# A graph layer with routed experts on one core: routing in two batches, results scattered to a two-row table

## The reference

```python
xs = x[src]
for r in range(4):                                   # relation weights
    msg += (xs @ W_rel[r] + b_rel[r]) * where(edge_type == r, edge_weight, 0)[:, None]
agg = segment_sum(msg, dst) / maximum(segment_sum(edge_weight, dst), 1)
x1  = layer_norm(x + x @ W_self + b_self + agg, ln1)
gnn = layer_norm(x1 + gelu(x1 @ W_ffn1 + b1) @ W_ffn2 + b2, ln2)     # 512 -> 1024 -> 512
x   = x + gnn                                        # gnn is fed the normed x

xt     = norm(x)
probs  = softmax(xt @ router_w.T + router_b)         # 16 experts, the best 2 are kept
out    = sum over e of gate[e] * (gelu(xt @ w1[e].T + b1[e]) @ w2[e].T + b2[e])   # 512 -> 256 -> 512
return x + out
```

## Time and profile before

| | us |
|---|---|
| median of three runs | 641.01 |
| the profiled execution | 639.41 |
| its span | 637.5 |
| PE busy in the span | 526.0 |
| DVE busy | 320.0 |
| POOL busy | 229.9 |
| ACT busy | 119.3 |

### The profile page before, as it was taken

One profiled execution on the slowest core, in us unless ns is written; L12 is line 12 of the kernel. 1 busy time (PEld: TensorE's weight loads), 2 busy tenths in 40 slices (PEclk: granted clock), 3 DMA queues, 4 the chain that ended last, 5 costly groups with the idle time before them and its releaser, 6 DMA issues.

```text
span 637.5 us, 7136 instructions
## 1 busy us (share of the span) xinstructions
PE 526.0 (82%) x2292; PEld 353.1 (55%) x2292; DVE 320.0 (50%) x847; ACT 119.3 (19%) x251; POOL 229.9 (36%) x270
## 2 busy tenths in 40 slices
PE   1999999999965999999999999529359999999300
PEld 1888888887612756656657667223146666666200
DVE  6788563212226145986977995948102222222144
ACT  2121101000111322322223312011022222222000
POOL 3630000037777777777773000004700011110273
PEclk9999999989977999999999999855569999999855
DMA  8427242249898677776774592442534477872285
GB/s 318 185 83 255 113 166 92 90 121 290 278 398 283 195 203 201 200 199 178 200 204 123 201 407 86 155 178 99 207 105 165 164 265 265 293 267 100 85 257 203
DMA packets 47703, 125.54 MB, mean 197 GB/s; under 512 B 6496, under 2 KB 7136, under 8 KB 45360
## 3 DMA queue, kind: packets, MB, share of 16 engines
q0 software_dynamic: 17344, 63.20, 32.3%
q1 hardware_dynamic: 27360, 57.57, 24.1%
q10 hardware_dynamic: 2960, 4.27, 2.3%
HBM read 85.70 MB, written 39.32 MB: 196 GB/s over the span
## 4 chain that ended last, share of the span: by engine, by line
PE 74%; POOL 8%; DVE 7%; issue 5%; DMA 4%; ACT 1%; POOLq 1%; ACTq 0%; SPq 0%; DVEq 0%
PE ps L828 11%; PE ps L839 10%; PE ps L961 8%; PE ps L978 8%; PE ps L762 7%; PE ps L763 7%; PE ps L764 7%; PE ps L794 6%; POOL greg L569 3%; POOL xslot L543 3%; PE ps L954 2%; POOL greg L522 2%; PE ps L805 2%; PE ps L860 1%; DMA x_res<-x 1%
## 5 line engine op out<-in xcount | busy, mean ns | idle before, releaser
L522 POOL DMA_INDIRECT greg<-msg,row_i x157 | 156.7, 998 | 145.0 <-DMA msg<-greg 93.6
L762 PE MATMUL ps<-w_hi,xT_hi 128*128 128x512 f32 x200 | 81.1, 405 | 0.0
L763 PE MATMUL ps<-w_lo,xT_hi 128*128 128x512 f32 x200 | 79.8, 399 | 0.0
L764 PE MATMUL ps<-w_hi,xT_lo 128*128 128x512 f32 x200 | 79.7, 398 | 0.0
L828 PE MATMUL ps<-freg,wreg 128*128 128x256 f32 x320 | 71.7, 383 | 0.8 <-ACT freg L622 0.8
L839 PE MATMUL ps<-wreg,freg 128*128 128x512 f32 x160 | 72.1, 598 | 0.0
L828 PEld LDWEIGHTS ps<-freg,wreg 128*128 128x128 f32 x320 | 60.3, 191 | 16.4 <-issue 7.5
L961 PE MATMUL ps<-wreg,freg 128*128 x224 | 55.7, 393 | 0.0
L978 PE MATMUL ps<-wreg,freg 128*128 x112 | 52.7, 593 | 0.9 <-ACT freg L709 0.9
L794 PE MATMUL ps<-greg,sel 128*32 128x512 f32 x320 | 47.9, 638 | 6.3 <-DMA greg<-msg,row_i 6.3
L543 POOL DMA_INDIRECT xslot<-work,pos_i x20 | 19.7, 986 | 85.2 <-DVE pos_i L1347 79.4
(11 more groups left out here) (170 smaller groups left out, 648.3 us busy)
## 6 DMA issues: line engine op xcount, KB each, us to landing
wreg<-experts POOLq DMA_DIRECT2D x11, 1025.0 KB, 6.3
msg<-greg SPq DMA_DIRECT2D x40, 256.0 KB, 2.0
xslot<-greg SPq DMA_DIRECT2D x1, 8960.0 KB, 25.6
greg<-xslot SPq DMA_DIRECT2D x28, 256.0 KB, 4.1
yslot<-greg SPq DMA_DIRECT2D x28, 256.0 KB, 2.9
wreg<-experts SPq DMA_DIRECT2D x5, 1025.0 KB, 9.6
wreg<-w SPq DMA_DIRECT2D x8, 512.0 KB, 12.7
w_in<-w_rel ACTq DMA_DIRECT2D x3, 1024.0 KB, 6.5
```

The source lines that it names most:

```text
L522: nc.gpsimd.indirect_dma_start(gath[:, c % RING, :], None, msg, bass.IndirectOffsetOnAxis(ap=row_i[:, c:c + 1], axis=0)).then_inc(s_gath[c ...
L762: nc.tensor.matmul(bank(t % 5), xT_hi[:, at], w_hi[:, i, wk], start=(k == 0), stop=False)
L763: nc.tensor.matmul(bank(t % 5), xT_hi[:, at], w_lo[:, i, wk], start=False, stop=False)
L764: mm = nc.tensor.matmul(bank(t % 5), xT_lo[:, at], w_hi[:, i, wk], start=False, stop=(k == KD - 1))
```

## The change

- **Routing** is split in `choose` and `place` and done in two batches, tiles 0 to 5 and tiles 6 to 9. The first batch's routing stands between `other_norms` of tile 7 and of tile 8 on DVE; its exp stands between `copy_xmT` of the fourth pair and `product_out` of tile 8 on ACT; its counts stand between the FFN products of tile 8 on PE. The best two are chosen on the logits, ahead of the exp. `place` takes a first layout of `xslot` from the first batch alone; rows of the second batch that don't fit go behind it. So a block's rows are no longer together, and DVE works out, per block, where its rows are (`trow_i`, from ten wide instructions and as many small ones on 128 partitions).
- **Rows of `xslot`** get four more values: the row's place in the result table, its first expert, and its two gates (`XW = 516`). `xslot` is cleared as soon as the gathers are issued, and one more DMA, behind the clearing, writes 4480 single ids of four bytes into it. `yslot` is gone, and its clearing with it.
- **Experts.** POOL loads each block's rows by an indirect gather (four blocks ahead) and, in place of the store, scatters the results, scaled by their gates on DVE, to a table `results` with two neighbouring rows per node. SP loads all expert weights. DVE works out gate and result row in four small instructions per block (`gates_of`).
- **Combine.** SP loads the results linearly, five loads of two tiles (1 MB); DVE adds both rows; ACT stores the output.
- **Bias product**: gates are turned in three groups with one copy each, and the product uses banks 0, 1, 2 and 4. It stands, as before, between routing and experts on PE. A small gelu on ACT after the exp loads its table early.
- **Nodes.** The bias of the second norm is added to `x_res` by POOL after the self bias (ten additions of 128x512), so that `other_norms` has one instruction less per tile. `sums_out` on ACT makes one copy in place of two, and DVE reads PSUM itself; `window_sums` waits for DVE's low part in place of the copies.
- **Start.** `turn_xn` runs two tiles ahead of the products in place of three.

The core of the diff:

```diff
+            def rows_to_tile(t):
+                if t >= MR:
+                    pool.wait_ge(e_xT, t - MR + 1)
+                    pool.wait_ge(e_prep, 2 * (t - MR + 1))
+                nc.gpsimd.indirect_dma_start(
+                    xs[:, t % MR, :], None, xslot,
+                    bass.IndirectOffsetOnAxis(ap=trow_i[:, t:t + 1], axis=0)).then_inc(e_x[t % MR], 16)
+
+            def tile_to_results(t):
+                pool.wait_ge(e_yt, t + 1)
+                nc.gpsimd.indirect_dma_start(
+                    results, bass.IndirectOffsetOnAxis(ap=node_i[:, t % MR:t % MR + 1], axis=0),
+                    ys[:, t % MR, :], None).then_inc(e_out[t % MR], 16)
+
+            def expert_tiles(first, end):
+                for t in range(first, min(first + AHEAD, end)):
+                    rows_to_tile(t)
+                for t in range(first, end):
+                    tile_to_results(t)
+                    if t + AHEAD < end:
+                        rows_to_tile(t + AHEAD)
+
+            pool.wait_ge(r_fast.sc, 2 * NT * 16)
+            pool.wait_ge(d_rows, 1)
+            expert_tiles(0, USUAL)
...
+            choose(r_fast, fast, cs, 0)
+            place(r_fast, cs, 0)
             other_norms(fast, cs, NT - 2)
             other_norms(fast, cs, NT - 1)
+            choose(r_fast, fast, cs, 1)
+            place(r_fast, cs, 1)
...
+            for g, (a, b) in enumerate(BIAS_TILES):
+                pe.wait_ge(d_gTc, g + 1)
+                for t in range(a, b):
+                    after(pe, d_b2t, t - len(B_BIAS) + 1)
+                    nc.tensor.matmul(bank(B_BIAS[t % len(B_BIAS)]), gT[:, t, :], eb2_s[:, :],
+                                     start=True, stop=True).then_inc(d_b2, 1)
             pe.wait_ge(d_b2t, NT)
...
+            for p in range(PAIRS):
+                sp.dma_start(both[:, 2 * p:2 * p + 2, :],
+                             results[4 * p * P:4 * (p + 1) * P, :].rearrange("(t p c) d -> p t (c d)", t=2, c=2))\
+                    .then_inc(f_in[p], 16)
...
+            for t in range(NT):
+                pool.wait_ge(s_xn, t + 1)
+                nc.gpsimd.tensor_tensor(x_res[:, t, :], x_res[:, t, :], vec[:, V_B2 - V_G1, :], ALU.add).then_inc(s_xb, 1)
```

More of the change, by code:

```diff
@@ new lines, in program @@
+        tval = room(TAB * EXPERTS).rearrange("p (t e) -> p t e", e=EXPERTS)
+        empty_slots = flat(tval)[:, 0:XW]
+        both = wreg[:, 0:2 * NT * D].rearrange("p (t n) -> p t n", t=NT)
+        tbase, texp, tstart, told, tfrom, tlater, tpos = (room(TAB) for _ in range(7))
+        tring = tfrom
+        slot_ids = tpos[:, 0:SLOT_TILES]
+        row16 = sb("row16", [P, 8, EXPERTS])
+        room_old, end_old, at_old, less, room_now, end_now, later_by, change_old = (row16[:, i, :] for i in range(8))
@@ L765, in product @@
                 mm.then_inc(s_prod, 1)
-            for t in range(3):
+            for t in range(2):
                 turn_xn(t)
@@ L905, in _ @@
             logits(fast, PAIRS - 1)
+            counts(r_fast, 1)
             with pe.If(general_wanted(pe)):
@@ L1173, in norm_stats @@
[L1173 to L1177 removed]
+                for s, r in enumerate(rows):
+                    n.did(v.bn_stats(st[:, s, :], r))
@@ new lines, in norm_stats @@
+                sync(n)
+                for s in range(k):
+                    n.did(v.bn_aggr(mv[:, s, :], st[:, s, :]))
+                sync(n)
+                var2, seed, sq, root = nvar[:, 0:k], nseed[:, 0:k], nsq[:, 0:k], nrs[:, 0:k]
+                did(v.tensor_scalar(var2, mv[:, 0:k, 1], EPS, None, ALU.add))
+                n.did(v.tensor_scalar(seed.bitcast(I32), var2.bitcast(I32), 1, None, ALU.logical_shift_right))
+                if k == 1:
+                    n.did(v.tensor_scalar(newton[:, :], nscale[:, :], var2, None, ALU.mult))
@@ new lines, in choose @@
+                did(v.tensor_tensor(lg[:, tiles, 0:EXPERTS], lg[:, tiles, 0:EXPERTS],
+                                    rb_s[:, :].unsqueeze(1).to_broadcast([P, k, EXPERTS]), ALU.add))
+                for t in range(a, z):
+                    n.did(v.max(lg[:, t, EXPERTS:], lg[:, t, 0:EXPERTS]))
+                sync(n)
+                v.tensor_tensor(low[:, tiles, :], lg[:, tiles, :],
+                                lg[:, tiles, EXPERTS:EXPERTS + 1].to_broadcast([P, k, EXPERTS + 8]),
+                                ALU.subtract).then_inc(r.low, 1)
@@ new lines, in choose @@
+                for t in range(a, z):
+                    n.did(v.max_index(i8[:, t, :], lg[:, t, EXPERTS:], lg[:, t, 0:EXPERTS]))
+                sync(n)
+                for c_ in range(2):
+                    n.did(v.tensor_copy(idx_f[:, c_, tiles], i8[:, tiles, c_]))
+                sync(n)
+                for c_ in range(2):
+                    n.did(v.tensor_tensor(choice[:, c_, tiles, :], num[:, 0:EXPERTS].unsqueeze(1).to_broadcast([P, k, EXPERTS]),
+                                          idx_f[:, c_, tiles].unsqueeze(2).to_broadcast([P, k, EXPERTS]), ALU.is_equal))
@@ L1286, in _ @@
                 for t in range(NT):
+                    zs.did(v.tensor_tensor(x_res[:, t, :], x_res[:, t, :], vec[:, V_B2 - V_G1, :], ALU.add))
+                sync(zs)
+                for t in range(NT):
                     after(dve, slow.x1T, t - 3)
@@ L1293, in _ @@
                         other_norms(slow, zs, t)
-                dve.wait_ge(slow.lgt, PAIRS)
+                dve.wait_ge(s_zero, 64)
+                for b in range(len(BATCHES)):
+                    choose(r_slow, slow, zs, b)
+                    place(r_slow, zs, b)
             rd = Steps(d_dve)
```

600 lines of the change are left out of this document (346 added, 254 removed).

## The result

| | before | after |
|---|---|---|
| median, us (4 runs each) | 640.51 | 655.13 |
| lowest to highest | 639.59 to 641.83 | 652.01 to 657.05 |
| ratio of the times, 95% interval | | 1.0222 (1.0177 to 1.0266) |
| span of the profiled execution | 637.5 | 655.3 |
| DVE busy in the span | 320.0 | 342.8 |

What follows compares the result with a forecast made beforehand. PE was taken to bound three quarters of the chain, nearly still before the first expert turn and after the last result. Terms 0.5 - 9.9 + 23.4 - 10.3 = +3.7 on span 637.5 led to 644.7 us, range 630 to 658.

Steps and rivals of the forecast that it cites:

- Start: First products: turning two ahead gains 0, POOL's ten additions slow DVE a little; +0.5 us, bounds 0 and 3.
- Node stage: Node products: DVE's shorter norms and the saved copy lie under a busy PE; 0 us.
- First batch: Routing of tiles 0 to 5: tile 8's norm starts at 401.4 in place of 398.45; scatters and clearing hidden.
- Second batch to T: Routing of tiles 6 to 9: rows known at T = 432.1, 4.7 us earlier than before.
- T to the first turn: Rows known to PE's first expert turn: bias product at half clock ends last, turn at T + 25; routing -9.9 us.
- Loop: Expert loop: take, scatter, gather and landing need 10.56 us for two iterations, where PE wants 8.22; +23.4 us.
- The pauses hide it in two of ten iterations: Expert loop: PE's existing pauses absorb part of the 1.17 us per tile, leaving 0.8 x 25 x 1.17.
- Combine: Last result to the end: linear loads in place of the old combine, E + 29.6 where it took 39.9; -10.3 us.
- The quick gather: Expert loop: gathers land at the scatter's 2.7 us, loop loses 8.4, 629.7 us; or not held, 621.3; chance 0.20.
- The full clock: Ahead of the experts: the bias product runs at full clock, 5 us less, 639.5 us; chance 0.12.
- Crowding: Expert loop: scatter and gather queue behind 1 MB of weights, landing 5.2 to 6.0, 655 to 664 us; chance 0.15.
- The slow ids: Routing: ids over 47 us hold both batches, 20 scatters stand in a row again, about 650 us; chance 0.03.

Runs made afterwards that it cites:

- start3: ctl with PE's turns of x_norm at the start three tiles ahead in place of two: 687.36 us, ratio 1.0179 to the kernel before.
- poollate: ctl with POOL's ten additions of the norm bias waiting until 30 of the 50 products are done: 692.92 us, ratio 1.0275 to the kernel before.
- fix3: fix2 with the expert bias product and its ten additions moved behind the expert tiles: 616.58 us, ratio 0.9655 to the kernel before.
- ctl: The change with two awaited register values written as the larger of value and 1, base of all experiments: 692.84 us on another chip, ratio 1.0263 to the kernel before.
- swap: ctl, still four tiles ahead, with POOL issuing the next gather before the result scatter: 626.32 us, ratio 0.98 to the kernel before.
- fix2: ahead5 and start3 in one: 623.63 us, ratio 0.9759 to the kernel before.
- ahead5: ctl with each expert tile's rows asked for five tiles ahead in place of four: 664.23 us, ratio 0.985 to the kernel before.
- fix4: fix3 with POOL's ten additions late, as in poollate: 615.35 us, ratio 0.9636 to the kernel before.
- fix3_early: fix3 with the flag that decides DVE's branch loaded ahead of the last two norms: 615.41 us, ratio 0.9619 to the kernel before.
- fix5: fix4 and fix3_early in one: 614.9 us, ratio 0.9607 to the kernel before.
- fix3_nobranch: fix3 without DVE's untaken branch to the general path and its contents: 616.04 us, ratio 0.9603 to the kernel before.
- ahead3: ctl with each expert tile's rows asked for three tiles ahead in place of four: 826.79 us, measured once.

## Why the prediction was right or wrong

- **Start, forecast +0.5, measured +4.7: the step that failed most for its size.** The text named both parts and priced them nearly at nothing: "Gain 0" for turning two ahead, and "DVE catches up within that stage" for the additions. start3 shows 2.6 us of PE's time for the first and poollate 1.8 for the second. The first product did start 1.9 us sooner (13.67 against 15.56), as said; what was missing is that a lead given up is paid for later, when DVE has a backlog: PE waited 2.06 and 1.71 us for DVE's additions at 44 and 52 us. The rule of the Trainium skill (SBUF — State Buffer, Who interferes with whom), that a DVE instruction with two SBUF inputs is held up by GpSimd reading SBUF, was set aside for the trace's x norms at 1.21 us; the one-hots, which have two such inputs, went from 426 to 1398 ns and from 416 to 950. Here the trace agrees with the page, and the bound of 3 us that came from it was nearer than my 0.5.
- **Node stage, 0.** Right: PE is busy 190 of 191 us.
- **First batch.** Tile 8's norm at 401.4; measured 405.88, that is 401.2 without the start's 4.7. The batch's scatters and the ids lay hidden, as forecast. A tile's norm took 8.97 us against 8.85.
- **Second batch to T, forecast 432.1;** measured 436.5, so 431.8. Right to 0.3 us.
- **T to the first turn, forecast 25 us, measured 27.9.** The bias product as the last to end was right, at half clock (12 matmuls in 10.57 us, 0.88 each, against 0.87), and so were the banks. The branch was mis-sized, 3.7 against 1.2, and since DVE's tables come behind it and the additions behind the tables, it must have gone through to the first turn; no run leaves the branch out with the bias product in front. fix3 gives the product's price: 10.6 us. That the data alone would allow T + 15.8 came near: fix3 turns at T + 17.1, because the last scatter goes out 0.6 us later than 1.27 apiece gives, and is seen as landed 4.0 us after its issue and not 2.7.
- **Loop, forecast +23.4, measured +33.7: the largest error in us.** The mechanism and the place were right, and so nearly was the landing: taken as 4.2 in the mean, measured 4.5 from issue to turn over the 16 tiles that PE waited for (3.28 to 7.12). What the sum has no term for is PE's clock. Over the loop PE stood still for 33.2 us in place of 9.5, +23.7; but the same 504 matmuls also took 10.1 us more of busy time, at a granted clock of 0.93 in place of 0.97. ctl, the same loop with 16 waits as well and nearly the same landings (4.4 in the mean), lost 26.9 us: +22.9 of standing still and +4.0 of busy time. The loops of the change and of ctl, in the columns of the earlier trace rows:

```profile
464.38:628.70 164.32, 131.14 (x504) 87.52 (x504) 45.01 (x168) 33.32 (x84) 49.95 (x51) 0.93 0.46 153
507.20:664.65 157.45, 125.05 (x504) 84.26 (x504) 45.04 (x168) 33.18 (x84) 50.12 (x51) 0.96 0.48 159
```

One place of it, in the change: behind its wait of 2.87 us PE turned tile 5 in 1.12 us where tile 4 took 0.66, and the first product behind the turn took 2.81 us where the one before took 1.90:

```profile
484.90 1.90 PE L1039 MATMUL ps<-wreg,freg 128*128 x8
...
492.51 2.81 PE L1039 MATMUL ps<-wreg,freg 128*128 x8
```

That the waits alone meet the forecast so closely is in part luck, since "The pauses hide it in two of ten iterations; over 25 iterations that is 0.8 x 25 x 1.17" isn't confirmed either. Between first and last take it is 149.3 us in the change and 143.0 in ctl, against 116.1 before, so 33.2 and 26.9 more for 27 tiles. 27 x 1.17 with nothing hidden gives 31.6, and with 0.8 of it 25.3: ctl is near the second and the change near the first, with the clock mixed into both. How much a pause of PE hides stays open.
- **Combine, forecast -10.3, measured -13.3.** The loads went out 3.9 us after the last take (4.6 forecast), the last landed 17.5 after that (18 forecast), and behind it came 5.2 us in place of 7.0.
- **The rivals.** The quick gather (0.20) is out: no tile that PE waited for was turned under 3.28 us after its gather's issue. The rule of the Trainium skill (DMA: Bandwidth & Descriptors, Anatomy of one DMA — SWDGE), 2.0 us and the bytes at 436 GB/s, gives 2.6; the trace doesn't agree for gathers (3.2 at least, 3.6 in the median) and does for the result scatters of the change (2.7 at least, 2.9 in the median; in swap the median is 4.9 and in fix2 3.9). The full clock is out: 0.88 us a matmul is what clock 0.50 gave before. Crowding (0.15) had its time, 655, right for the wrong cause: the landings were 4.5 us in the mean and not 5.2 to 6.0, and ahead5 and swap move as many bytes in less time and lose 24 to 30 us of loop. The slow ids are out.

The four terms together: 4.2 too little at the start, 2.5 at the routing, 10.3 in the loop (10.1 of it PE's busy time at the lower clock), and 3.0 the other way at the combine, from +3.7 to +17.8. With the prediction's own sum the change would have been a small loss; as it stands, one number, AHEAD, or the order of two calls on POOL turns a loss of 2.2% into a gain of 1.5 to 2%.

## What to carry to other kernels

Where a load is issued behind a store that waits for a result, write the circle down (take, store issue, load issue, landing, use, next take) and divide it by the tiles it is shared by; if that is more than the engine's own time per tile, ask for the data one tile sooner, or issue the load ahead of the store, before doing anything else. Give the clock of the engine that waits a term of its own: in this loop the same matmuls took 4 to 10 us longer once PE waited for most of its tiles. An engine's lead over another that looks unused at the start is what pays for the other's backlog a few tiles on, and work put in front of a loop "while one waits anyway" is free only as long as nothing on its own chain (a late table, four banks, half clock) outlasts the wait.

## What the runs showed of the hardware that was not expected

- Beside POOL's additions of 128x512, DVE's instructions of 128x256 with two SBUF inputs took 1398 and 950 ns in place of 426 and 416, and one of 128x2048 took 3383 in place of 2292.
- A branch of DVE over a large body that isn't entered cost 3.6 to 4.1 us in ten kernels (3.65 in fix3, 3.76 in fix4); with the flag loaded earlier it is 2.71 and 2.91 (fix3_early, fix5).
- POOL's scatters are slower beside DVE's wide table instructions: 0.97 us each without, 1.06 to 1.32 with. In fix3 DVE works on its tables of 576 from 439.2 on and the scatters from the fifth on are slow; in fix3_nobranch DVE comes to them 4 us sooner and the first five take 1.03 to 1.32 us, the last three again 0.97 to 0.99. One of each, fix3's seventh and fix3_nobranch's:

```profile
442.53 1.28 POOL L565 DMA_INDIRECT xslot<-rows_w,pos_i  x1 [0.30 <-issue]
```
```profile
443.00 0.97 POOL L565 DMA_INDIRECT xslot<-rows_w,pos_i  x1 [0.30 <-issue]
```

- With PE waiting at each tile (ahead3) the granted clock was 0.77 to 0.80 in three stretches of 30 us; in the change's loop 0.93, in ctl's, the same loop, 0.96, in the loop before 0.97. The lowest goes with the most busy time for the same 504 matmuls: 131.1, 125.1 and 121.1 us.
